# Five of the eight shared-expert groups of expert layer B computed in the last two turns of phase A, and rows of their own for empty gather places

## The reference

```
# first layer (attention with a wide, 64-number head), then the gated narrow attention, then
x = x + tanh(g_xattn[1]) * narrow_attention(layernorm(x), ctx)
# expert layer "B": one shared expert for all tokens, one routed expert each
h = layernorm(x)
shared = (silu(h @ shared_gate_w) * (h @ shared_up_w)) @ shared_down_w      # inner size 512
logits = h @ gate_w;  e = argmax(logits);  s = sigmoid(max(logits))
routed = (silu((h*s) @ routed_gate_w[e]) * ((h*s) @ routed_up_w[e])) @ routed_down_w[e]
x = x + tanh(g_ffn[1]) * (shared + routed)
# ... two more layers and a further attention (phase C) ...
# expert layer "D": the same form, four of 32 experts for each token, inner size 128
```

## Time and profile before

| what | before |
|---|---|
| median of 3 runs (lowest, highest) | 4536.08 us (4534.49, 4537.32) |
| the profiled execution | 4539.24 us, span 4537.5 us |
| mean granted clock of TensorE | 0.958 |
| TensorE, VectorE, ScalarE, GpSimd busy | 90%, 51%, 39%, 21% of the span |
| phase A's last routing step | 2475 us |
| phase B: first shared matmul, first block | 2485 us, 2659 us |
| phase D: block loop | 4084 to 4368 us |

### The profile page before, as it was taken

How to read it: one execution, slowest core, us unless ns; L and a number is a source line. 1 busy time by engine, 2 the same in 40 slices (tenths; PEclk the granted TensorE clock), 3 DMA queues, 4 the chain that set the end, 5 groups by cost and what they waited for, 6 DMA issues and landing times. The chain is left out here.

```text
span 4537.5 us, 77340 instructions
## 1 busy us (share of the span) xinstructions
PE 4085.1 (90%) x29123; PEld 2852.1 (63%) x29168; DVE 2300.1 (51%) x7126; ACT 1777.0 (39%) x3733; POOL 944.8 (21%) x1113
## 2 busy tenths in 40 slices
PE   7999999999999999999975999968889888669986
PEld 4666666666666666666653589965666665448854
DVE  4555665556555655556543222124566666473345
ACT  4445554554545554555422111112444343313320
POOL 2221222212221222212210011111000000005557
PEclk9999999999999999999976999987999999879998
DMA  3000000000000000000001149950000000029964
GB/s 109 3 3 6 8 8 6 3 8 8 6 5 6 8 8 3 6 8 6 6 3 61 58 152 336 326 186 12 17 22 22 20 20 10 12 91 375 378 195 128
DMA packets 132652, 300.85 MB, mean 66 GB/s; under 512 B 19968, under 2 KB 86080, under 8 KB 123712
## 3 DMA queue, kind: packets, MB, share of 16 engines
q1 hardware_dynamic: 80976, 216.67, 13.3%
q0 software_dynamic: 18336, 50.09, 3.8%
q10 hardware_dynamic: 32976, 29.13, 1.9%
HBM read 245.76 MB, written 50.07 MB: 65 GB/s over the span
## 5 line engine op out<-in xcount | busy, mean ns | idle before, releaser
L420 POOL TENSOR_SCALAR a_wide_p<-a_wide_p,a_w_inv 128x512 f32<-128x512 f32 x512 | 354.9, 706 | 1430.2 <-DVE a_w_inv L1007 1430.2
L813 ACT ACTIVATE a_wide_p<-a_wide_p,a_row_min 128x512 f32<-128x512 f32 x512 | 363.5, 712 | 6.0 <-DVE a_row_min L1002 2.8
L1077 DVE TENSOR_REDUCE a_q_pad<-ring 128x4 f32<-128x1024 f32 x256 | 301.3, 1219 | 105.3 <-PE ring L630 103.4
L1002 DVE CUSTOM_DVE_ANT_0 a_wide_p<-ring,a_neg_keys 128x512 f32<-128x512 f32 x434 | 285.0, 687 | 124.9 <-PE ring L504 124.5
L504 PE MATMUL ring<-a_qk 64*128 64x512 f32 x868 | 288.5, 640 | 19.6 <-DVE a_wide_pt L1012 15.5
L861 ACT ACTIVATE a_probs<-ring 128x1024 f32<-128x1024 f32 x256 | 250.4, 1018 | 80.4 <-PE ring L644 80.4
L1467 PE MATMUL ring<-b_xgt,b_we 128*128 128x128 f32 x2016 | 235.8, 275 | 2.6 <-issue 2.2
L1467 PEld LDWEIGHTS ring<-b_xgt,b_we 128*128 128x128 f32 x2016 | 230.1, 192 | 3.7 <-issue 3.0
L2439 DVE CUSTOM_DVE_ANT_0 c_junk<-ring,c_neg_mask 128x256 f32<-128x256 f32 x512 | 182.6, 420 | 97.1 <-PE ring L2006 96.5
L534 PE MATMUL ring<-a_wide_pt,a_v 128*64 128x256 f32 x1792 | 219.5, 387 | 0.0
L512 PEld LDWEIGHTS ring<-a_wkv,a_kv_t 128*128 128x128 f32 x1568 | 185.0, 192 | 20.0 <-issue 12.3
(11 more groups left out here) (429 smaller groups left out, 8446.8 us busy)
## 6 DMA issues: line engine op xcount, KB each, us to landing
b_we<-in_experts SPq DMA_DIRECT2D x63, 1536.0 KB, 9.6
d_we<-in_experts SPq DMA_DIRECT2D x159, 384.0 KB, 6.2
d_results<-d_yb ACTq DMA_DIRECT2D x159, 128.0 KB
b_results<-b_yb ACTq DMA_DIRECT2D x63, 128.0 KB, 9.4
a_cb<-in_ctx SPq DMA_DIRECT2D x16, 256.0 KB, 2.8
b_turned<-a_heads_t SPq DMA_DIRECT2D x16, 256.0 KB, 2.4
b_rows<-a_heads SPq DMA_DIRECT2D x16, 256.0 KB, 2.2
b_xt<-b_turned SPq DMA_DIRECT2D x8, 512.0 KB, 10.1
```

What stands on the lines that cost most here:

```text
L420: ins = pool.tensor_scalar(wide_p[:, h % 4, t, :], wide_p[:, h % 4, t, :], w_inv[:, t, h:h + 1], 1.0, ALU.mult, ALU.mult)
L813: ins = act.activation(wide_p[:, h % 4, t, :], wide_p[:, h % 4, t, :], ACT.Exp, scale=-1.0, bias=row_min[:, h, t:t + 1], accum_out=row_sum ...
L1002: dve.tensor_tensor_reduce(wide_p[:, h % 4, t, :], wbank(name), neg_keys[w % 2][:], -0.125, 3.0e38, ALU.add, ALU.min, row_min[:, h, t:t + ...
L1077: dve.tensor_reduce(q_pad[:, :, 2 * i:2 * i + 2, HD].rearrange("p t h -> p h t"), s, AX.X, ALU.max, negate=True).then_inc(nr.taken(name), 1)
```

## The change

The work of groups 0 to 4 of layer B's shared expert is cut into 60 units: for each group and n = 0 .. 3 a gate unit ("sg", two matmul instructions of 512 columns), an up unit ("su", the same) and, a group later, a down unit ("dn", four instructions of 256 columns). The places 4 .. 39 of turn 16 and 0 .. 23 of turn 17 are 60 as well, and each takes one unit, behind the narrow steps of the place and on each engine. The units take banks of the `wr` rotation. Their weights and tokens are loaded over the weights of phase A that are done with (`wkv`, `wq`), by SP at the start of turns 16 and 17. ScalarE computes a tanh of half the gate output in place of the Silu, and VectorE makes silu(g) * u from it in two operations (`(tanh + 1) * g`, then `* 0.5 * u`), and adds the down outputs to x. Phase B computes groups 5 to 7, of which 5 and 6 stand beside the search; layer D keeps all its groups (`first` = 0).

In both expert layers an empty place now gets a row of its own: real tokens are coded so that their sum is never 0, and where the sum is 0 the index is n + 24 p for place p of block n.

```diff
 PAIRS = HEADS // 2
+TAIL = 5
...
+                units = []
+                for g in range(TAIL + 1):
+                    for n in range(4):
+                        units += [("sg", g, n), ("su", g, n)] * (g < TAIL) + [("dn", 4 * (g - 1) + n)] * (g > 0)
+                places = [(B, p) for p in range(4, 40)] + [(B + 1, p) for p in range(24)]
+                fill = {place: units[len(units) * n // len(places):len(units) * (n + 1) // len(places)] for n, place in enumerate(places)}
+
+                def filled(i, p):
+
+                    return fill.get((i, p), [])
...
                         w_order += [("S", i, u, 0, j) for j in range(2)] * on(i) + [("K", nw, nu)] * on(nw)
-                        w_order += [("wo", i - 1)] * (u == 1 and on(i - 1))
-                        w_order += [("S", i, u, 1, j) for j in range(2)] * on(i) + [("Q", nw, nu)] * on(nw)
+                        w_order += [("wo", i - 1)] * (u == 1 and on(i - 1)) + filled(i, 5 * u)
+                        w_order += [("S", i, u, 1, j) for j in range(2)] * on(i) + [("Q", nw, nu)] * on(nw) + filled(i, 5 * u + 1)
                         w_order += [("V", i, u)] * on(i)
-                        w_order += [("lT", i + 1)] * (u == 6 and on(i + 1))
+                        w_order += [("lT", i + 1)] * (u == 6 and on(i + 1)) + filled(i, 5 * u + 2)
                         w_order += [("AV", bw, bu)] * on(bw)
-                        w_order += [("xT", i + 1)] * (u == 6 and on(i + 1))
-                        w_order += [("PT", i, u, t, h) for t in range(2) for h in range(2)] * on(i)
+                        w_order += [("xT", i + 1)] * (u == 6 and on(i + 1)) + filled(i, 5 * u + 3)
+                        w_order += [("PT", i, u, t, h) for t in range(2) for h in range(2)] * on(i) + filled(i, 5 * u + 4)
...
+                    ws_loaded = [sem(ctx, f"a_ws_loaded{i}") for i in range(2)]
+                    xt_loaded = [sem(ctx, f"a_xt_loaded{i}") for i in range(2)]
+                    s_turned = sem(ctx, "a_s_tanh_ready")
...
+                    ws = wkv[:].rearrange("p c n -> p (c n)")
+                    xt = [wq[:, g, :].rearrange("p (c n) -> p c n", c=C) for g in range(2)]
+                    s_tanh = wide_pt[:].rearrange("p h k n -> p (h k n)").rearrange("p (s n) -> p s n", s=4)
+                    hidden = wide_p[:].rearrange("p h t n -> p (h t n)").rearrange("p (s i n) -> p s i n", s=2, i=4)
...
+                        def tokens(g):
+                            if g >= 2:
+                                wr.wait_full(sp, ("su", g - 2, 3))
+                            sp.dma_start(xt[g % 2], rb.turned[:, :, 512 * g:512 * g + 512]).then_inc(xt_loaded[g % 2], 16)
+
                         for i in range(B + 2):
                             c0 = i - 2
+                            if i == B:
+                                wr.wait_full(sp, ("V", B - 1, PAIRS - 1))
+                                sp.wait_ge(e_turned_stored, 16 * (B - 2))
+                                sp.dma_start(ws[:, 0:2048], a["shared1"][:, 0:2048]).then_inc(ws_loaded[0], 16)
+                                tokens(0)
+                                sp.dma_start(ws[:, 2048:3072], a["shared1"][:, 2048:3072]).then_inc(ws_loaded[1], 16)
+                                tokens(1)
+                                tokens(2)
+                            if i == B + 1:
+                                for g in range(3, TAIL):
+                                    tokens(g)
                             if on(c0):
                                 vr.wait_taken(sp, ("eT", c0))
                                 sp.dma_start(rb.turned[:, :, 256 * c0:256 * c0 + 256], heads_t[:]).then_inc(e_turned_stored, 16)
...
+                        def shared(i, p):
+                            for name in filled(i, p):
+                                wr.wait_room(pe, name)
+                                if name[0] == "dn":
+                                    g, t = name[1] // 4, name[1] % 4
+                                    pe.wait_ge(ws_loaded[1], 16)
+                                    for n in range(4):
+                                        wr.wait_taken(pe, ("su", g, n))
+                                    for n in range(4):
+                                        ins = pe.matmul(wbank(name)[:, 0:256], hidden[:, g % 2, n, P * t:P * t + P],
+                                                        ws[:, 2048 + D * n:2048 + D * n + D], start=(n == 0), stop=(n == 3))
+                                else:
+                                    g, n, w0 = name[1], name[2], 1024 * (name[0] == "su")
+                                    pe.wait_ge(ws_loaded[0], 16)
+                                    pe.wait_ge(xt_loaded[g % 2], 16 * (g // 2 + 1))
+                                    for c in range(C):
+                                        ins = pe.matmul(wbank(name), ws[:, w0 + 512 * c + P * n:w0 + 512 * c + P * n + P], xt[g % 2][:, c, :],
+                                                        start=(c == 0), stop=(c == C - 1))
                                 ins.then_inc(wr.full(name), 1)
...
+                        def shared_tanh(i, p):
+                            for name in filled(i, p):
+                                if name[0] == "sg":
+                                    n = 4 * name[1] + name[2]
+                                    wr.wait_full(act, name)
+                                    if n >= 4:
+                                        wr.wait_taken(act, ("sg", name[1] - 1, name[2]))
+                                    act.activation(s_tanh[:, n % 4, :], wbank(name), ACT.Tanh, scale=0.5).then_inc(s_turned, 1)
...
+                        def shared_taken(i, p):
+
+                            for name in filled(i, p):
+                                if name[0] == "dn":
+                                    t = name[1]
+                                    wr.wait_full(dve, name)
+                                    dve.scalar_tensor_tensor(out=x_all[:, t, :], in0=wbank(name)[:, 0:256], scalar=gates[:, 5:6], in1=x_all[:, t, :],
+                                                             op0=ALU.mult, op1=ALU.add).then_inc(wr.taken(name), 1)
+                                if name[0] == "su":
+                                    g, n = name[1], name[2]
+                                    h = hidden[:, g % 2, n, :]
+                                    dve.wait_ge(s_turned, 4 * g + n + 1)
+                                    if g >= 2:
+                                        wr.wait_full(dve, ("dn", 4 * (g - 2) + 3))
+                                    dve.scalar_tensor_tensor(out=h, in0=s_tanh[:, (4 * g + n) % 4, :], scalar=1.0, in1=wbank(("sg", g, n)),
+                                                             op0=ALU.add, op1=ALU.mult).then_inc(wr.taken(("sg", g, n)), 1)
+                                    wr.wait_taken(dve, ("sg", g, n))
+                                    wr.wait_full(dve, name)
+                                    dve.scalar_tensor_tensor(out=h, in0=h, scalar=0.5, in1=wbank(name), op0=ALU.mult, op1=ALU.mult).then_inc(wr.taken(name), 1)
...
                                 beside(i, 5 * u)
+                                shared_taken(i, 5 * u)
                                 if on(i):
                                     mask_scores(i, u, 1)
                                     invert_sums(i, u, 0)
                                 beside(i, 5 * u + 1)
...
+                spare = s_("spare", [P, NB])
+                found = s_("found", [P, 3, NB])
...
-                ring_order = [("sgu", u, i) for u in range(early) for i in range(4)] + [("x", 0)]
+                ring_order = [("sgu", u, i) for u in range(first, early) for i in range(4)] + [("x", 0)]
...
-                        for u in range(G):
+                        for u in range(first, G):
                             sp.dma_start(xt[:, :, 512 * u:512 * u + 512], r.turned[:, :, 512 * u:512 * u + 512]).then_inc(xt_loaded[u], 16)
-                            if u == 0:
+                            if u == first:
...
+                        pool.iota(spare[:], [[1, NB]], base=-T * P // 2, channel_multiplier=T - 8, allow_small_or_imprecise_dtypes=True).then_inc(consts, 1)
...
-                                pe.wait_ge(xt_loaded[n // 4], 16)
-                            shared_in(n // 4, n % 4)
+                                pe.wait_ge(xt_loaded[first + n // 4], 16)
+                            shared_in(first + n // 4, n % 4)
...
-                        for u in range(2, early + 2):
+                        for u in range(first + 2, early + 2):
...
-                            dve.wait_ge(consts, 4)
+                            dve.wait_ge(consts, 5)
...
+                            dve.scalar_tensor_tensor(out=token[:], in0=token[:], scalar=0.0, in1=token[:], op0=ALU.is_ge, op1=ALU.add)
...
```

(38 more changed lines are left out.)

8 lines of the change are left out of this document (added).

## The result

| what | before | after |
|---|---|---|
| median of 4 runs each (lowest, highest) | 4536.70 us (4534.49, 4537.62) | 4436.82 us (4433.21, 4440.65) |
| the profiled execution, its span | 4539.24, 4537.5 us | 4433.61, 4431.9 us |
| mean granted clock of TensorE | 0.958 | 0.971 |

The ratio is 0.9781, 95% interval 0.9764 to 0.9798: 100 us faster, where 4438 was forecast.

The account below looks back on a forecast made before the run. At phase A's end no engine is full and a chain of small steps binds; phase B's shared part is bound by TensorE, loop D by transfers. -103.2 + 25 - 20 - 1.5 + 0.7 = -99.0 gives 4438 us, own range 4420 to 4455.

Parts of the forecast that it names:

- Removed from phase B: Phase B's shared part: five groups of four iterations at 5.16 us leave the path, -103.2 us.
- The tail: End of phase A, turns 16 and 17: 60 added units lengthen it by 25 us, between +13 and +44.
- the walk: Phase A's last two turns, place by place, narrow steps at 2.4 GHz, longer engine queue counted: eight stretches sum to +23.4 us.
- the check by TensorE alone: End of phase A: narrow steps 64 us plus units 103 make 167 in a 154 us stretch, at least +13.
- ScalarE's tables: Phase A's end: tanh between exponentials needs no table load, 0 us; with two loads per tanh at most +20.
- Queues: SP's new loads ahead of stores in turns 16 and 17, and weight and token transfers, delay nothing: 0 us.
- The gathers: Block loop D: with rows of their own all 159 blocks go at 1.66 us, -20 us, bounds 0 and -24.
- The argument from empty blocks: Loop D's last 16 blocks are empty and read row 2048 everywhere; slow packets (339 against 113 ns) stand exactly there.
- Block loop B: Layer B's block loop, bound by TensorE, gains between 0 and -3 us from own rows, taken as -1.5.
- The small operations: Both expert layers: a GpSimd constant and a small VectorE operation ahead of the search, about 0.35 us each, +0.7.
- The rivals: Whole kernel: own rows bring nothing (0.12), narrow steps keep the low clock (0.08), nothing hidden (0.05), slower than before (0.03).
- the slower case: Phase A's tail: TensorE stays at 1.2 GHz, units included, tail +147 us, total 4559 us; chance 0.03.

Follow-up runs that it names:

- fillers: Kernel before plus 49 extra matmuls of 0.86 us, result unread, in phase A's tail, nothing moved: 4519.0 us, ratio 0.9960.
- six groups: Changed kernel with six groups instead of five moved into phase A's tail: 4443.4 us, ratio 0.9790 to the kernel before.
- the nine and the three traces: Traces of kernels with empty places' rows at a pitch of 24 (nine) or on row 2048 (three): loop D means 260.8 and 281.1 us.
- the better order: Changed kernel with three or six groups, tanh behind the narrow exponentials at two places: 4458.1 us (three); 4438.8 us, ratio 0.9783 (six).

## Why the prediction was right

**Removed from phase B**: 103.2 forecast, 103.4 measured. The three groups left were enough to cover the gathers and weights: the block loop starts without a wait, right behind the last shared output (2564.95 + 13.98 us; first turned block 2578.76). That block starts 80.7 us earlier than before, where about 78 was forecast.

**The tail**: +25 taken, +23.4 by the walk, +24.4 measured from the last step ahead of place 4's unit (2322.07 before, 2320.33 after) to phase B. Phase B begins only 22.6 us later because the trace of after reached that step 1.7 us earlier, ahead of the first unit. Stretch by stretch, in the order of the walk, forecast and measured (from the steps shown above and the earlier trace rows): +2.3 and +2.5; +3.2 and +2.8; +1.7 and +1.4; -2.6 and -2.2; +4.2 and +4.6; -2.5 and -1.7; +11.3 and +11.1; +5.8 and +5.9. The step that carried it was taking every narrow step at 2.4 GHz: they take 65 us in the trace of after, where the check by TensorE alone had 64. The fillers show that the clock is a cause: their 42 us shortened the tail. The Trainium skill, "TensorE: Matmul & The Clock Gate" (Part 1), has the low level as the default that activity lifts; the fillers agree (0.70 to 0.99 up to 2460 us). The walk was right for the order of units that five groups give. It looked at ScalarE's and VectorE's queues for what a place adds, but not at whether a unit's tanh stands ahead of exponentials that are ready; with six groups that order costs 8.3 us.

**ScalarE's tables**: taken as 0, none seen: tanh stands 20 times among the exponentials of the tail and no table load between them. The one load there (2501.3) is that of phase B's Silu, which the kernel before has too (2478.8). The Trainium skill, "ScalarE: Activation LUTs" (Table sets), has tanh in the set of exp; the trace agrees.

**Queues**: 0, and no wait on weights or tokens stands among TensorE's waits of the tail.

**The gathers**: -20 taken, -21.5 between the two traces shown, -20.2 between the means of the nine and the three traces. The runs with rows alone are 18 to 20 us faster in all, loop B included. The argument from empty blocks was right; whether part-empty blocks gain too can't be told at this spread (259.1 to 264.5).

**Block loop B**: -1.5 taken, -3.1 measured, just beyond its bound of -3; the traces with row 2048 have 338.0 to 339.2 us and those with rows of their own 336.1 to 336.7, so -1.3 to -3.1. The small operations, +0.7, can't be read from these traces: the stretch from loop B to loop D alone takes 1076.6 to 1086.3 us in the fourteen.

**The rivals**: none came about. The rows alone gave 18 to 20 us, the narrow steps ran at 1.00, and of the units' 103 us some 79 were hidden or won back by the clock. Even six groups, with more work in the tail, is 95 us faster than before (4443.4 against 4538.3), far from the slower case.

One caution on this agreement: the errors are of both signs, and the spread between executions (2 to 7 us from the start alone, and 259.1 to 264.5 us for loop D) is as large as any of them. The mechanism stands by the stretches; that the medians (99.9 us apart) meet the forecast of 99.0 within 1 us is partly luck.

## What to carry to other kernels

Where an engine order of small dependent steps leaves TensorE short gaps and its granted clock is low, moving independent TensorE work into the gaps pays twice, and the price of each portion rises (here 1.3 us for the first three groups together with the better order, then 9, 13 and 18.5 against 20.6 saved) until the next one is worth next to nothing. Before placing it, write down each engine's order at each place: a portion's step on ScalarE ahead of a critical one makes the chain wait for the portion's matmul. Padding in an indirect gather should point at different rows, not at one.

## What the runs showed of the hardware

- Matmuls without use made the kernel faster: 42 us of them on TensorE took 18.5 us off a stretch of 159 by raising the granted clock (0.70 to 0.99 between 2320 and 2460 us).
- An indirect gather whose 128 places read one 1 KB row takes 308 to 363 ns a packet at the end of loop D and 199 to 254 at the end of loop B, against 108 to 118 for different rows; one row a block takes 119 in D and 204 in B. The cause within the memory or the queue was not looked for.
- The granted clock also dips between 120 and 160 us in six of the fourteen traces (0.91, once 0.96), where TensorE is busy for 36.7 of 40 us with or without the dip, and the tail of phase A then starts 2 to 7 us later. What brings the dip was not looked for.
